# Layer 1 of a two-layer graph network: 64-row products in pairs, slice sums in four 64x64 quadrants, features moved to VectorE

## The chip, the cores and the metric

One NeuronCore of a Trainium2 chip runs the kernel. The metric is the device time in microseconds (us), median over the runs. The profile is of one execution, and its span runs from the first to the last instruction of that execution. Five engines matter: PE (TensorE), DVE (VectorE), ACT (ScalarE), POOL (GpSimd) and SP (SyncE, which only issues DMAs).

## The reference, cut to what matters

```python
# x (100000, 32), 25000 edges (src, dst), edge_weight, edge_attr_3
x = layernorm(x + L0(x, ...))            # scatter messages both ways, four tanh layers
x = layernorm(x + L1(x, edge_weight, edge_attr_3, edge_index))

def L1(features, abs_distances, rel_vec, edge_index, w1, b1, w2, b2):
    R = relu(abs_distances[:, None] @ w1 + b1) @ w2 + b2      # (E, 64) @ (64, 384): radial products
    Y = spherical_harmonics(rel_vec)
    Fj = features[src]                                        # 8 scalars and 8 vectors a row
    # for every block (i, j) and every k: sum over the 8 input channels v
    acc += NORM[i] * einsum('euv,ef,evi,ofi->euo', R[..., k], Y[lf], Fj[j], C)
    out = zeros.at[dst].add(msg)
```

## The kernel before, in words

The 25000 edges are padded to 196 tiles of 128 edges, one edge a partition. The stages before Layer 1 sort the edges, gather rows for Layer 0, walk the sorted tiles and run the four tanh layers. They end with x1, the input of Layer 1, stored to DRAM. After Layer 1 a last walk adds the first messages of each window of nodes, normalizes and stores.

Layer 1 takes the tiles in 28 groups (`NU`) of 7 (`U`). Each engine runs its own list in program order, and semaphores join the lists. For a group g:

- SP loads `arow` (each edge's weight, broadcast to 64 partitions), `load_weights`. ACT makes `ht` from it by one Relu, `hidden_3` (L738). A 65th row of `ht` is constantly 1.
- POOL gathers 7 times 128 rows of x1 by indirect DMA into `gat1`, `gather_3` (L566). It stands up to three groups ahead, as there are three buffers.
- ACT spreads the gathered rows into `feat5`, `fd` and `fk`, `features_3`. POOL makes three small products of `feat5` with the edge's direction, its own `features_3` (L577 to L579), and DVE reduces one and subtracts the others, `features_3` (L1389, L1390).
- PE makes the radial products: a tile is one product of `ht` (65 rows x 128 edges) with `rw` (65 x 384; row 65 is the bias), `radial` (L1018). Three PSUM banks take turns. ACT copies each to `rsb`, `radial_3`. There is one `rsb`, so the copies for group g+1 wait for DVE's products of group g.
- DVE multiplies `rsb` with `fd` and `fk`, `products_3` (L1397, and L1400 three times), into `prod`: 16 slices of 280 columns (7 tiles x 40).
- PE adds the 16 slices: 16 products of the 128x128 identity with a slice, accumulated in one bank of two, `sums` (L1025).
- ACT copies the sum out, `sums_3`. DVE builds the centred message and its payload, `message_3` (L1408 to L1420). PE multiplies it with the one-hot `oh1` that ACT makes (`away_from_3` L764, `hot_3` L769), `extras` (L1034). DVE adds the 7 results to `res`, `extras_3` (L1308).

The orders of the lists are: PE `radial(g+1)`, `sums(g)`, `extras(g-1)`; DVE `products_3(g)`, `features_3(g+1)`, `message_3(g-1)`, `extras_3(g-2)`; ACT `features_3(g+1)`, `radial_3(g+1)`, `away_from_3(g)`, `hidden_3(g+2)`, `hot_3(g)`, `sums_3(g)`.

An f32 product is one instruction in the program and two weight loads and two MATMUL records in the trace; a bf16 product is one of each.

## Time and profile before

| | |
|---|---|
| median of 3 runs | 1983.5 us (1983.34 to 1989.6) |
| the profiled execution, from first to last instruction | 1707.1 us |
| lies outside the profiled instructions (median less span) | 276.4 us |
| PE busy | 1315.9 us, 77% |
| DVE busy | 1193.5 us, 70% |
| POOL busy | 1068.9 us, 63% |
| ACT busy | 858.9 us, 50% |
| mean granted TensorE clock | 0.846 |

The profiled execution is known by its span alone. The rest of the measured time lies before the first and behind the last instruction, and a difference in the span is read as the same difference in the time. Busy shares are means over stages with different limits, so the rows below are taken by stretches. Layer 1 runs from about 1140 to 1560 us of the span. PE's clock has two levels, 2.4 GHz (1.00 in the rows) and 1.2 GHz (0.50), and a number between is a mean over a stretch.

### The profile page before, as it was taken

What the parts mean: (1) busy time and instruction counts of PE and PEld (TensorE: products, weight loads), DVE (VectorE), ACT (ScalarE), POOL (GpSimd) and SP (SyncE); (2) the same over time, 40 slices, a digit from 0 to 9 for tenths busy, and PEclk for the clock granted to TensorE, in tenths of its full rate; (3) what the DMA queues carried; (4) which work ended last, traced back from release to release, by engine and by line L of the source; (5) the groups of instructions that cost most, each with busy time, mean ns of one, the idle gap of its engine ahead of it and who ended that gap; (6) DMA issues with size and microseconds to landing.
All of it is one profiled execution on the core that took longest, in us unless ns stands there. A gap on an engine that the chain in (4) does not pass through costs nothing.

```text
span 1707.1 us, 25367 instructions
## 1 busy us (share of the span) xinstructions
PE 1315.9 (77%) x6200; PEld 957.6 (56%) x6200; DVE 1193.5 (70%) x3648; ACT 858.9 (50%) x2256; POOL 1068.9 (63%) x1168
## 2 busy tenths in 40 slices
PE   5699993686513777665778999958999999996673
PEld 1388881242212555554655666635777777775563
DVE  9699995677512443676667999964777777774776
ACT  0167770011101222666775777735666666664884
POOL 7777778777777777774111444448877887830444
PEclk8599996577555999888888999977999999997655
DMA  1000000123224988665555666531222222213785
GB/s 41 13 14 13 14 14 20 47 72 79 67 68 127 257 250 246 171 174 145 132 138 140 179 184 189 163 95 32 58 58 57 58 64 67 59 42 78 196 216 157
DMA packets 298498, 178.98 MB, mean 105 GB/s; under 512 B 28715, under 2 KB 290032, under 8 KB 298352
## 3 DMA queue, kind: packets, MB, share of 16 engines
q1 hardware_dynamic: 219712, 116.54, 26.0%
q0 software_dynamic: 29008, 36.18, 8.3%
q10 hardware_dynamic: 49632, 24.65, 5.0%
q8 instruction: 51, 0.84, 0.2%
q14 instruction: 95, 0.78, 0.2%
HBM read 111.18 MB, written 66.07 MB: 104 GB/s over the span
## 4 chain that ended last, share of the span: by engine, by line
PE 42%; POOL 28%; issue 16%; DVE 8%; DMA 2%; DVEq 2%; SPq 1%; ACT 1%; POOLq 0%; ACTq 0%
PE bank L1025 12%; POOL gat L511 12%; POOL lined L518 11%; PE bank L994 7%; PE bank L1018 7%; DVE res L1308 5%; PE bank L945 3%; POOL out L591 3%; PE bank L947 3%; PE bank L1034 3%; PE bank L1003 3%; PE bank L987 3%; DMA placed<-pay,pos_i 1%; DVEq L1308 1%; DVEq L1302 1%
## 5 line engine op out<-in xcount | busy, mean ns | idle before, releaser
L566 POOL DMA_INDIRECT gat<-x_d,src_i x196 | 253.2, 1292 | 59.0 <-issue 53.1
L511 POOL DMA_INDIRECT gat<-in_x,key_i x196 | 211.1, 1077 | 64.8 <-issue 62.4
L1308 DVE TENSOR_TENSOR res<-res,bank 128x128 f32 x588 | 168.4, 286 | 108.5 <-issue 24.4
L528 POOL DMA_INDIRECT placed<-pay,pos_i x196 | 191.9, 979 | 68.1 <-issue 65.6
L518 POOL DMA_INDIRECT lined<-in_x,other_i x196 | 195.8, 999 | 59.7 <-issue 59.7
L1025 PE MATMUL bank<-prod,ident 128*128 128x280 f32 x896 | 217.0, 400 | 0.0
L1025 PEld LDWEIGHTS bank<-prod,ident 128*128 128x128 f32 x896 | 171.0, 191 | 46.5 <-issue 0.6
L956 PE MATMUL bank<-woh,pw 128*128 128x128 f32 x784 | 135.4, 335 | 69.3 <-DVE woh L1287 33.4
L956 PEld LDWEIGHTS bank<-woh,pw 128*128 128x128 f32 x784 | 120.3, 238 | 85.5 <-DVE woh L1287 44.5
L56 ACT ACTIVATE xt<-bank 128x128 f32<-128x128 f32 x98 | 26.6, 271 | 269.6 <-PE bank L897 261.2
L1018 PE MATMUL bank<-rw,ht 65*128 65x384 f32 x392 | 141.3, 514 | 23.3 <-ACT ht L738 13.8
L553 POOL TENSOR_TENSOR hx<-hid,xin 128x512 f32<-128x512 f32 x49 | 62.0, 1264 | 136.2 <-ACT hid L724 136.2
L878 PE MATMUL bank<-tile_oh,sel 128*128 128x196 f32 x784 | 143.0, 337 | 3.1 <-ACT tile_oh L651 2.0
L878 PEld LDWEIGHTS bank<-tile_oh,sel 128*128 128x128 f32 x784 | 131.0, 193 | 17.3 <-issue 17.0
L1130 DVE SCALAR_TENSOR_TENSOR junk<-iota,w_f,bank 128x196 f32<-128x196 f32 x392 | 138.0, 408 | 0.9 <-PE bank L869 0.9
L994 PE MATMUL bank<-hid,wsl 128*128 128x512 f32 x294 | 134.9, 594 | 0.4 <-ACT hid L724 0.4
L56 ACT ACTIVATE rsb<-bank 128x384 f32<-128x384 f32 x196 | 95.5, 491 | 52.7 <-PE bank L1018 45.6
L1052 PE MATMUL bank<-pw,oh 128*128 128x128 f32 x392 | 89.6, 400 | 41.3 <-ACT oh L814 39.9
L689 ACT ACTIVATE woh<-iota,kr 128x128 f32<-128x128 f32 x294 | 93.8, 390 | 52.6 <-PE bank L956 26.0
L1018 PEld LDWEIGHTS bank<-rw,ht 65*128 65x128 f32 x392 | 75.8, 200 | 75.0 <-issue 17.9
L724 ACT ACTIVATE hid<-bank,bias 128x512 f32<-128x512 f32 x147 | 101.1, 688 | 31.2 <-PE bank L994 31.2
L1138 DVE TENSOR_TENSOR pay<-bank,wjs 128x512 f32<-128x512 f32 x49 | 33.8, 689 | 115.1 <-PE bank L902 115.0
(204 smaller groups left out, 2840.5 us busy)
## 6 DMA issues: line engine op xcount, KB each, us to landing
pw<-placed SPq DMA_DIRECT2D x588, 68.0 KB, 2.1
pw<-placed SPq DMA_DIRECT2D x98, 272.0 KB
xin<-in_x_t SPq DMA_DIRECT2D x53, 256.0 KB, 3.2
placed<-pay SPq DMA_DIRECT2D x49, 272.0 KB, 2.4
x_d<-res POOLq DMA_DIRECT2D x49, 256.0 KB, 3.8
placed<-pay SPq DMA_DIRECT2D x28, 448.0 KB, 3.2
out<-out ACTq DMA_DIRECT2D x49, 256.0 KB, 2.7
xin<-in_x_t ACTq DMA_DIRECT2D x45, 256.0 KB, 3.6
```

The costliest lines, as they stand in the source:

```text
L56: return act.activation(out, in_, ACT.Copy)
L511: pool.indirect_dma_start(gat[:, t, :], None, x, bass.IndirectOffsetOnAxis(ap=key_i[:, 0, t:t + 1], axis=0)).then_inc(s_gat, 16)
L518: pool.indirect_dma_start(lined[i % LINED][:, k, :], None, x, bass.IndirectOffsetOnAxis(ap=other_i[:, t:t + 1], axis=0)).then_inc(s_lined[ ...
L528: pool.indirect_dma_start(placed[1].rearrange("t p r -> (t p) r"), bass.IndirectOffsetOnAxis(ap=pos_i[:, 1, t:t + 1], axis=0), pay[i % 4][ ...
L566: pool.indirect_dma_start(gat1[g % 3][:, k, :], None, x1_d, bass.IndirectOffsetOnAxis(ap=src_i[:, t:t + 1], axis=0)).then_inc(c_gat[g % 3] ...
L878: ins = pe.matmul(psum[4 + 2 * v][:, 0:NT], sel[g % 2][:, k, v, :], tile_oh[g % 2][:, k, :], start=t == 0, stop=t == NT - 1)
L956: ins = pe.matmul(quarter(bank, k), pw[i % 6][:, k, 0:P], woh[i % 4][:, k, :], start=True, stop=True)
L994: pe.matmul(psum[BANK[n][h]][:, :], wsl[:, 2 + n, :], hid[n - 1][h][:, :], start=True, stop=True).then_inc(m_mm[n], 1)
L1018: pe.matmul(psum[n % 3][:, 0:RC], ht[g % 2][:, P * k:P * k + P], rw[:, :, :].rearrange("p a b -> p (a b)"), start=True, stop=True).then_in ...
L1025: ins = pe.matmul(psum[3 + g % 2][:, 0:40 * U].rearrange("p (t u) -> p t u", t=U), ident[:, :], prod[g % 2][:, :, v, :], start=v == 0, sto ...
L1130: dve.scalar_tensor_tensor(out=junk[n % 4][:, :], in0=iota[:, :], scalar=w_f[:, c, t:t + 1], in1=column(n), op0=ALU.is_equal, op1=ALU.mult ...
L1308: add.up(dve.tensor_tensor(into, into, quarter(bank + k // G, k % G), ALU.add))
```

## The change

The change touches Layer 1 and what feeds it.

- `arow`, `ht`, `rw` and the radial weights now stand on 128 partitions: even tiles of a group on partitions 0 to 63, odd ones on 64 to 127. `ht` is 128 x 512 instead of 64 x 896. The bias has no row of its own. It is split in three bf16 pieces, which lie on three rows of each half of `rb3`, and each tile gets one extra bf16 product of ones with `rb3` ahead of its f32 product. Four banks take turns.
- Each 128x128 identity product over a slice becomes two of the four 64x64 products: for a row half a and a column half b, the slice v + (a != b) goes to bank `SUMS[a]`, partitions of half b. What belongs to half a but landed on the other half is copied out by ACT (`crossed`) and brought back by two more 64x64 products, `cross`, which stand behind `extras(g-1)` on PE. Both banks belong to one group, so `sums(g)` waits for the copies of group g-1 rather than of g-2.
- POOL's three feature products move to DVE.
- DVE prepares `rb3` in the placement stage, where it already made `rw`. SP loads the weights of `rw` behind a wait for `s_rec`.

```diff
-            for g in range(NU + 1):
-                if g < NU:
-                    gather_3(g)
-                if g >= 1:
-                    features_3(g - 1)
+            for g in range(NU):
+                gather_3(g)
...
-                act.activation(ht[h][0:HID, :], arow[h][:, :], ACT.Relu, bias=rwc_sb[:, 1:2], scale=rwc_sb[:, 0:1]).then_inc(c_ht, 1)
+                act.activation(ht[h][:, :], arow[h][:, :], ACT.Relu, bias=rwc_sb[:, 1:2], scale=rwc_sb[:, 0:1]).then_inc(c_ht, 1)
...
             def sums_3(g):
                 act.wait_ge(c_sum, g + 1)
+                for a in range(2):
+                    ins = act_copy(act, crossed[HALVES[1 - a], :, :], summed(a, 1 - a))
+                ins.then_inc(c_cross, 1)
+                act.wait_ge(c_whole, g + 1)
                 wait(act, c_msg, g)
-                ps = psum[3 + g % 2][:, 0:40 * U].rearrange("p (t u) -> p t u", t=U)
-                act_copy(act, msg[:, :, 0:8], ps[:, :, 0:8])
-                act_copy(act, rest[:, :, :], ps[:, :, 8:40]).then_inc(c_scal, 1)
+                for a in range(2):
+                    act_copy(act, msg[HALVES[a], :, 0:8], summed(a, a)[:, :, 0:8])
+                    ins = act_copy(act, rest[HALVES[a], :, :], summed(a, a)[:, :, 8:40])
+                ins.then_inc(c_scal, 1)
...
             def radial(g):
                 pe.wait_ge(c_ht, g + 1)
-                for k in range(U):
-                    n = U * g + k
-                    wait(pe, c_rsb, n - 2)
-                    pe.matmul(psum[n % 3][:, 0:RC], ht[g % 2][:, P * k:P * k + P], rw[:, :, :].rearrange("p a b -> p (a b)"),
-                              start=True, stop=True).then_inc(c_r, 1)
+                for k in range(0, U, 2):
+                    pair = [(U * g + k + o, HID * o) for o in range(min(2, U - k))]
+                    for n, r in pair:
+                        wait(pe, c_rsb, n - 3)
+                        pe.matmul(psum[RADIAL[n % 4]][:, 0:RC], unit[r:r + HID, :], rb3[r:r + HID, :, :].rearrange("p a b -> p (a b)"),
+                                  start=True, stop=False)
+                    for n, r in pair:
+                        pe.matmul(psum[RADIAL[n % 4]][:, 0:RC], ht[g % 2][r:r + HID, P * (k // 2):P * (k // 2) + P],
+                                  rw[r:r + HID, :, :].rearrange("p a b -> p (a b)"), start=False, stop=True).then_inc(c_r, 1)
...
             def sums(g):
                 pe.wait_ge(c_prod, g + 1)
-                wait(pe, c_scal, g - 1)
-                for v in range(16):
-                    ins = pe.matmul(psum[3 + g % 2][:, 0:40 * U].rearrange("p (t u) -> p t u", t=U), ident[:, :], prod[g % 2][:, :, v, :],
-                                    start=v == 0, stop=v == 15)
+                wait(pe, c_scal, g)
+                for v in range(0, 16, 2):
+                    for b in range(2):
+                        for a in range(2):
+                            ins = pe.matmul(summed(a, b), ident[HALVES[a], HALVES[a]], prod[g % 2][HALVES[a], :, v + (a != b), :],
+                                            start=v == 0, stop=v == 14 and a != b)
                 ins.then_inc(c_sum, 1)
+            def cross(g):
+                pe.wait_ge(c_cross, g + 1)
+                for a in range(2):
+                    ins = pe.matmul(summed(a, a), ident[HALVES[1 - a], HALVES[1 - a]], crossed[HALVES[1 - a], :, :], start=False, stop=True)
+                ins.then_inc(c_whole, 1)
...
             def features_3(g):
                 h = g % 2
...
+                dve.wait_ge(c_feat, g + 1)
+                chain.up(dve.tensor_tensor(dprod[:, :, :, :], feat5[h][:, :, :, 0:3], along(0), ALU.mult))
+                chain.up(dve.tensor_tensor(kp[:, 0], feat5[h][:, :, :, 2:5], along(1), ALU.mult))
+                dve.tensor_tensor(kp[:, 1], feat5[h][:, :, :, 1:4], along(2), ALU.mult).then_inc(c_kp, 1)
+                done(chain)
+                dve.tensor_reduce(fd[h][:, :, 1, :], dprod[:, :, :, :], AX_X, ALU.add)
                 dve.wait_ge(c_kp, g + 1)
-                dve.tensor_reduce(fd[h][:, :, 1, :], dprod[:, :, :, :], AX_X, ALU.add)
```

PE's list before, from `radial(0)` on (`bank<-rw,ht` is a radial product, `bank<-prod,ident` a slice of the sums, `bank<-pay,oh` the extras):

```order
L1018 MATMUL bank<-rw,ht 128x384 x14
L1025 MATMUL bank<-prod,ident 128x280 x16
L1018 MATMUL bank<-rw,ht 128x384 x7
L1025 MATMUL bank<-prod,ident 128x280 x16
L1034 MATMUL bank<-pay,oh 128x128 x7
```

PE's list now, the whole of one later group (`bank<-rb,unit` is the bias, `bank<-crossed,ident` the halves brought back):

```order
L1032 MATMUL bank<-rb,unit 128x384 x2
L1035 MATMUL bank<-rw,ht 128x384 x2
L1032 MATMUL bank<-rb,unit 128x384 x2
L1035 MATMUL bank<-rw,ht 128x384 x2
L1032 MATMUL bank<-rb,unit 128x384 x2
L1035 MATMUL bank<-rw,ht 128x384 x2
L1032 MATMUL bank<-rb,unit 128x384
L1035 MATMUL bank<-rw,ht 128x384
L1044 MATMUL bank<-prod,ident 64x280 x32
L1059 MATMUL bank<-pay,oh 128x128 x7
L1051 MATMUL bank<-crossed,ident 64x280 x2
```

A group's 7 radial and 16 sum products became 14 and 32, and two products that wait for ACT stand at its end, ahead of the next group's radial products.

ACT's list now, from the one-hot of group g to the features of g+2 (before, the five rows from `crossed` to `rest` were the two copies `msg<-bank 128x7x8` and `rest<-bank 128x224`, and `ht` was 64x896):

```order
L778 ACTIVATE oh<-oh 128x896
L56 ACTIVATE crossed<-bank 64x280 x2
L56 ACTIVATE msg<-bank 64x7x8
L56 ACTIVATE rest<-bank 64x224
L56 ACTIVATE msg<-bank 64x7x8
L56 ACTIVATE rest<-bank 64x224
L56 ACTIVATE feat<-gat 128x56x3
L56 ACTIVATE feat<-gat 128x56x2
L56 ACTIVATE fd<-gat 128x7x8
L56 ACTIVATE fk<-gat 128x7x8 x3
L56 ACTIVATE rsb<-bank 128x384 x7
```

The wait for PE's `cross` lies between `crossed` and the first `msg`, and the features and the `rsb` copies of the next groups are queued behind it.

DVE's list now, between the products of two groups:

```order
L1462 TENSOR_TENSOR prod<-rsb,fk 128x112x8 x3
L1446 TENSOR_TENSOR dprod<-feat,rec 128x168
L1447 TENSOR_TENSOR kp<-feat,rec 128x168
L1448 TENSOR_TENSOR kp<-feat,rec 128x168
L1450 TENSOR_REDUCE fd<-dprod 128x7x8
L1452 TENSOR_TENSOR fk<-kp 128x7x8x3
L1470 TENSOR_TENSOR rq<-rest,rec 128x168
```

The three rows L1446 to L1448 are the ones that stood on POOL; before, L1389 (the reduction) followed `prod` directly.

## Rows read from the trace of the kernel before

**Rows 1.** Stretch: us, busy (count) of PE, PEld, DVE, ACT, POOL; PEclk, DMA, GB/s.

```profile
1200.00:1500.00 300.00, 300.00 (x1322) 226.69 (x1321) 220.69 (x399) 194.91 (x529) 237.82 (x221) 1.00 0.25 60
```

**Rows 2.** Chain that ended last, one group of Layer 1: start, us, what.

```profile
1269.88 7.55 PE bank L1025 x32
1277.42 1.56 PE bank L1034 x14
1278.98 4.52 PE bank L1018 x14
```

**Rows 3.** Waits, 1180 to 1540 us: total, times, longest.

```profile
ACT msg L56 <- PE bank L1025: 87.1, 27, 4.2
DVE fd L1389 <- POOL kp L579: 58.5, 26, 6.4
```

**Rows 4.** Timeline of DVE, one group: start, us, what.

```profile
1280.61 0.33 DVE L1389 TENSOR_REDUCE fd<-dprod 128x56 f32<-128x168 f32 x1 [1.93 <-POOL kp L579]
1280.85 0.43 DVE L1390 TENSOR_TENSOR fk<-kp 128x168 f32<-128x168 f32 x1
1281.13 0.31 DVE L1408 TENSOR_TENSOR rq<-rest,rec 128x168 f32<-128x168 f32 x1
...
1284.50 2.86 DVE L1308 TENSOR_TENSOR res<-res,bank 128x128 f32 x7 [0.70 <-issue]
1287.28 2.02 DVE L1397 TENSOR_TENSOR prod<-rsb,fd 128x1792 f32<-128x1792 f32 x1
1289.22 3.09 DVE L1400 TENSOR_TENSOR prod<-rsb,fk 128x896 f32<-128x896 f32 x3
1294.22 0.33 DVE L1389 TENSOR_REDUCE fd<-dprod 128x56 f32<-128x168 f32 x1 [1.91 <-POOL kp L579]
```

**Rows 5.** Timeline of PE at full clock in the sort, bf16 products.

```profile
183.26 0.33 PE L868 MATMUL bank<-oh,lower 128*128 128x392 bf16 x1
183.42 0.33 PE L869 MATMUL bank<-cum,pick 113*128 113x392 bf16 x1
```

**Rows 6.** Timeline of ACT, one group.

```profile
1277.46 0.22 ACT L56 ACTIVATE msg<-bank 128x56 f32<-128x56 f32 x1 [3.15 <-PE bank L1025]
1277.58 0.35 ACT L56 ACTIVATE rest<-bank 128x224 f32<-128x224 f32 x1
1277.81 0.57 ACT L56 ACTIVATE feat<-gat 128x168 f32<-128x168 f32 x2
...
1278.37 0.61 ACT L56 ACTIVATE fk<-gat 128x56 f32<-128x56 f32 x3
...
1282.25 0.49 ACT L56 ACTIVATE rsb<-bank 128x384 f32<-128x384 f32 x1 [0.15 <-PE bank L1018]
...
1283.93 2.14 ACT L764 ACTIVATE oh<-iota,kr 128x128 f32<-128x128 f32 x7
1285.97 1.12 ACT L738 ACTIVATE ht<-arow,rwc_sb 64x896 f32<-64x896 f32 x1
1287.00 0.94 ACT L769 ACTIVATE oh<-oh 128x896 f32<-128x896 f32 x1
```

**Rows 7.** Group of POOL's gathers, 1202 to 1529.3 us: busy, mean ns, idle before.

```profile
L566 POOL DMA_INDIRECT gat<-x_d,src_i x159 | 212.0, 1333 | 45.0 <-issue 42.7
```

**Rows 8.** Chain that ended last, start of Layer 1.

```profile
1163.60 2.02 DVE prod L1397
...
1174.69 8.61 PE bank L1025 x32
```

**Rows 9.** Chain that ended last, end of Layer 1.

```profile
1537.89 7.56 PE bank L1025 x32
...
1552.44 3.31 PE bank L1034 x14
```

**Rows 10.** Stretches in a walk of Layer 0 and in the placement, as in rows 1.

```profile
840.00:900.00 60.00, 42.16 (x234) 35.71 (x233) 41.05 (x147) 43.30 (x116) 9.79 (x56) 0.84 0.53 133
450.00:600.00 150.00, 64.72 (x295) 43.34 (x292) 45.15 (x154) 21.61 (x86) 113.90 (x118) 0.67 0.52 142
```

More of the change, by code:

```diff
@@ L147, in gnn_kernel @@
         bias = sb("bias", [P, 4])
-        rwc_sb = sb("rwc_sb", [HID, 2])
-        rw = sb("rw", [HID + 1, 16, 24])
+        rwc_sb = sb("rwc_sb", [P, 2])
+        rw = sb("rw", [P, 16, 24])
+        rb3 = sb("rb3", [P, 16, 24], BF16)
+        unit = sb("unit", [P, P], BF16)
         kr = sb("kr", [P, NT])
@@ L241, in gnn_kernel @@
         rest = sb3("rest", [P, U, D])
+        crossed = sb3("crossed", [P, U, 40])
         mean = sb3("mean", [P, U])
@@ L411, in gnn_kernel, with summed @@
         BACK = (5, 6, 7)
+        RADIAL = (0, 1, 2, 7)
+        SUMS = (3, 4)
+        HALVES = [slice(HID * a, HID * a + HID) for a in range(2)]
+        def summed(a, b):
+            return psum[SUMS[a]][HALVES[b], 0:40 * U].rearrange("p (t u) -> p t u", t=U)
         block = ctx.enter_context(nc.Block())
@@ L423, in _ @@
             sp.dma_start(bias[:, :], b0).then_inc(s_wld, 16)
-            sp.dma_start(rwc_sb[:, :], rwc).then_inc(s_wld, 16)
-            sp.dma_start(rw_raw[:, :], rwb).then_inc(s_wld, 16)
+            for h in range(2):
+                sp.dma_start(rwc_sb[HID * h:HID * h + HID, :], rwc).then_inc(s_wld, 16)
             sp.wait_ge(s_zero, 1)
@@ L432, in load_x @@
                 sp.dma_start(wins(xin[n % 4][:, :]), x_t[G * b:G * b + G].rearrange("w p q -> p w q")).then_inc(s_xin[n % 4], 16)
+            sp.wait_ge(s_rec, 1)
+            for h in range(2):
+                sp.dma_start(rw_raw[HID * h:HID * h + HID, :], rwb[0:HID, :]).then_inc(s_rwld, 16)
+                sp.dma_start(rb_raw[HID * h:HID * h + HID, :], rwb[HID:HID + 1, :].partition_broadcast(HID)).then_inc(s_rwld, 16)
             for q in range(NG):
@@ L479, in load_weights @@
                 wait(sp, c_ht, g - 1)
-                sp.dma_start(arow[h][:, :].rearrange("p (t q) -> p t q", t=U),
-                             ew_d[U * g:U * g + U, :].partition_broadcast(HID)).then_inc(c_arow[h], 16)
+                for o in range(2):
+                    n = (U + 1 - o) // 2
+                    sp.dma_start(arow[h][HID * o:HID * o + HID, 0:P * n].rearrange("p (t q) -> p t q", t=n),
+                                 ew_d[U * g + o:U * g + U:2, :].partition_broadcast(HID)).then_inc(c_arow[h], 16)
             def store_3(g):
@@ L1044, in _ @@
                     extras(g - 1)
+                if g < NU:
+                    cross(g)
             pe.wait_ge(c_scal, NU)
@@ new lines, in radial_weights @@
+            def radial_weights():
+                dve.wait_ge(s_rwld, 64)
+                dve.memset(unit[:, :], 1.0)
+                chain.up(combine(rw, rw_raw))
+                done(chain)
+                chain.up(combine(rb, rb_raw))
+                chain.up(dve.tensor_scalar(half[:, :], pcol[:, :], float(HID), -float(HID), ALU.is_ge, ALU.mult))
+                done(chain)
+                chain.up(dve.tensor_tensor(half[:, :], half[:, :], pcol[:, :], ALU.add))
+                done(chain)
+                for n in range(3):
+                    chain.up(dve.tensor_scalar(piece[:, n:n + 1], half[:, :], float(n), None, ALU.is_equal))
+                for n in range(3):
+                    chain.up(dve.tensor_copy(rb_h[:, :, :], rb[:, :, :]))
+                    done(chain)
+                    if n == 0:
+                        ins = dve.tensor_scalar(rb3[:, :, :], rb_h[:, :, :], piece[:, 0:1], None, ALU.mult)
+                    else:
+                        ins = dve.scalar_tensor_tensor(out=rb3[:, :, :], in0=rb_h[:, :, :], scalar=piece[:, n:n + 1], in1=rb3[:, :, :],
+                                                       op0=ALU.mult, op1=ALU.add)
+                    if n == 2:
+                        ins.then_inc(s_rw, 1)
+                    else:
+                        chain.up(ins)
+                        chain.up(dve.tensor_tensor(rb[:, :, :], rb[:, :, :], rb_h[:, :, :], ALU.subtract))
+                        done(chain)
```

73 lines of the change are left out of this document (36 added, 37 removed).

## The prediction, made before the result was known

> **What bounds the kernel now.** I read first the busy time by stretch. In Layer 1 PE is busy for all of 300 us at full clock, DVE for 220.7, ACT for 194.9, POOL for 237.8 [rows 1]. Since a busy PE can hide waits, I then took the chain that ended last: through all of Layer 1 it holds only PE's rows, 7.55 us of slice sums, 1.56 us of extras, 4.52 us of radial products, without a gap, 13.63 us a group [rows 2]. The waits say the same from the other side: ACT waits 87.1 us for the sums, DVE 58.5 us for POOL's feature products [rows 3]. Last, the timelines of the three others give what each needs of the 13.6 us once PE no longer sets them [rows 4, 6, 7]. Everything outside Layer 1 stays, so the question is the period of a group, times the 27 periods between the products of group 0 and of group 27.
>
> PE's prices are spacings, not the recorded durations: an f32 record of 280 columns takes 7.55 / 32 = 0.236 us, one of 384 takes 4.52 / 14 = 0.323 us [rows 2], a bf16 record of 392 takes 0.165 us although it is shown with 0.33 [rows 5].
>
> **PE, part by part.** Two 64-row products stand on different rows of the array, four 64x64 products on different quarters. No row of this kernel shows two products at once in parts of the array, so the price of a part has two ends: a share of a full record (0.236 / 4 = 0.059 us for a quarter's record, 0.323 / 2 for a half's), or the full record.
> - Sums: 32 products, 64 records. At 0.059 that is 3.8 us (saves 3.8), at 0.236 it is 15.1 us (costs 7.6).
> - Radial: 7 f32 products, now 4 turns instead of 7. A turn is 0.165 for the bias and 2 x 0.323, so 0.81, four are 3.2 us (saves 1.3); with no overlap 7 x 0.81 = 5.7 us (costs 1.2).
> - Cross: 2 products, 2 x 0.236 = 0.47 us if they overlap, 0.94 if not.
> - Changes of the array's division, four a group: between nothing and the 0.165 us by which a record outlasts its spacing [rows 5], so 0 to 0.7 us; I take 0.5.
>
> With full overlap PE works 3.2 + 3.8 + 1.56 + 0.47 + 0.5 = 9.5 us a group, and is no longer the bound. I take full overlap, since each of the four products in a turn has its own rows or columns, its own bank or its own half of one, and 64 columns of weights in place of 128.
>
> **DVE.** From the reduction at 1280.61 to the last of the prod rows at 1289.22 + 3.09 = 1292.31 there is no wait but 0.70 us of issue: 11.70 us. Then it waits 1.91 us for POOL, and the period is 13.61 us [rows 4]. The wait goes; three products of 168 columns come. The nearest rows are 0.31 and 0.43 us long for 168 columns, and follow each other by 0.24 and 0.28 us [rows 4]. Three take between 0.72 and 1.3 us. I take 0.9. DVE needs 11.7 + 0.9 = **12.6 us** a group. This is late next.
>
> **ACT and the loop through PE.** A group's `rsb` copies start at a moment X, when DVE's products end. PE has four banks full, and needs copies 0 and 1 (0.49 us each [rows 6]) for its next pair: that ends at X + 1.0 + 0.8, the last single at X + 2.6, the sums at X + 6.5, extras at X + 8.0. ACT meanwhile: 7 copies to 3.6, one-hot 2.14 to 5.7, `ht` with 512 columns instead of 896, about 0.7, to 6.4, the Relu 0.94 to 7.4 [rows 6]. `crossed` is two copies of 280 columns, between the 0.35 of 224 and the 0.49 of 384, less overlap, 0.7: X + 8.1. PE's cross and its result 0.6: 8.7. The halved `msg` and `rest` take twice the 0.35 us of today, since a copy's columns and not its partitions count: 9.4. Features 1.17 us (1277.81 to 1278.98 [rows 6]): 10.6, with the 0.5 us of changes about **11.1 us**. Only then may the next `rsb` copies start. That is 1.5 us under DVE's 12.6, so the added wait is hidden as long as the sums take no more than 3.8 + 1.5 = 5.3 us; from 6.3 us on the period is longer than today's.
>
> **POOL.** 7 gathers of 1.333 us and 0.30 of issue are 11.4 us [rows 7]; the three feature products leave. The gathers are stretched beside DVE's products; were all of DVE's new 0.9 us added to them, 12.3, still under 12.6. SP's two loads in place of one are issued in time it idles.
>
> **The clock.** PE waits about 3 us a group now. In a walk where PE is busy 42.2 of 60 us, its mean clock is 0.84, so a third of the stretch ran at 1.2 GHz [rows 10]. PE would be busy 9.5 / 12.6 = 75% here. A third of a period at half clock adds up to 2.1 us to PE's part of the loop, 11.1 to 13.2, and nothing if it falls where PE is ahead. I take 0.3 us on the period: **12.9 us** (ends 12.6 and 13.5).
>
> **Ends of the stage, and the rest.** The first products stand behind POOL's features, which stand behind the gathers of group 1; they start at 1163.60 [rows 8]. DVE alone can start when the `rsb` copies are in, some 3 us earlier (0 to 3.5). At the end 7.56 us of sums start 1 us after the products [rows 9]; now 3.8, then extras, cross and copies: 2 us less (0 to 3). DVE's preparation of `rb3` is about 25 small instructions, at most 12 us, in a stretch of 150 us in which DVE works 45 and POOL 114 [rows 10]: POOL's DMAs hide it; zero. Uncovered it would cost those 12 us.
>
> **Sum.** (13.63 - 12.9) x 27 = 19.7, plus 3, plus 2 = 24.7 us. The span goes from 1707.1 to 1682.4. The median stands 276.4 us above the span, and nothing there changes, so 1983.5 - 24.7 = **1959 us**. This case's own range: at 12.6, 27.8 + 6.5 = 34 less, 1949; at 13.4, with 3 of gain at the ends, 1974.
>
> **Rivals.**
> 1. *Only neighbours overlap* (slower). An f32 product is two records on the same part of the array. If PE starts its records strictly in program order, the second record of a product waits for its first, and the next product's first starts beside it: one f32 product per 0.236 us, whatever the number of parts. 32 products take 7.55 us, the same as today, and the loop is X + 2.9 for radial (a pair is 0.165 + 3 x 0.323), 10.4 for the sums, 11.2 `crossed`, 12.0 extras, 12.9 cross (3 x 0.236 and the result), 13.6 the copies, 14.8 the features, 15.2 with changes. (15.2 - 13.63) x 27 = 42 us, less 2 at the ends: **2024 us**. For it: the doubled records [rows 2] are back to back and every product here has two; against it: nothing shows yet that a record on another part must wait. It decides from sums of 6.3 us on. The Trainium skill, "TensorE: Matmul & The Clock Gate", Part 3, says that MATMULs start and end in program order, and only weight loads are pulled ahead; by that rule, applied to two-record products, this rival would hold. The same section gives 4 tiles about 3 times the throughput, for products that are not doubled. No run here shows either yet.
> 2. *No overlap at all* (slower): radial tail 3.3, sums 15.1, then cross, copies and features as above, 23 us a group: 9.4 x 27 = 253, **2235 us**. For it: every record of today's trace on one engine is a full turn; against it: the parts share neither rows, columns nor bank.
> 3. *The clock eats it* (no change). PE's waits bring it to half clock just where the sums start; the loop becomes 13.5 to 14 us. At 13.8: 4.6 more, 5 less at the ends, **1983 us**. For it: rows 10. Against: a slow PE waits less, and today's Layer 1 came back to full clock after the 8.61 us sums of its start [rows 8] and stayed there [rows 1].
> 4. *Partial overlap*: sums of 6.5 to 7 us by weight loads that don't hide (64 loads now for 32). Loop near 14.2: 15 us more, less 5: **1994 us**.
>
> **Chances.** Forecast 0.48, rival 1 0.27, rival 2 0.06, rival 3 0.10, rival 4 0.09. A difference of under 0.3%, 6 us, can't be told from none. Faster by more: the forecast and a share of rival 3, 0.51. Within 0.3%: 0.07. Slower: 0.42. The range reaches from the forecast's lower end, 1949, to rival 1 with half a period's 0.3 us on top, 2032; it leaves out rival 2 and little else.
>
> **What would show it.** PE's records of a sum phase: 64 within 3.8 us (forecast) or 7.5 (rival 1) or 15. A DVE without waits between its groups and a period of 12.6 to 12.9, against ACT's `rsb` copies waiting no longer for DVE but following its features directly, with DVE waiting for `rsb` (rivals 1 to 4). PEclk under 0.9 in Layer 1 for rival 3. First products near 1160. If DVE's three products take over 1.3 us or the gathers over 1.8 us each, the forecast fails without PE.

## The result, and what it depends on

| | before | changed | ratio, 95% interval |
|---|---|---|---|
| the comparison that scores the prediction | 1986.55 us | 2062.62 us | 1.0392 (1.0376 to 1.0408) |
| the same two kernels on another chip | 1704.38 us | 1659.53 us | 0.9732 (0.9715 to 0.9748) |

The change was forecast at 1959 us and came out at 2062.62 us: slower by 3.9%. (One of the four runs of the kernel before, of 2395.32 us, was slow and does not count in the ratio.) On another chip the change is faster by 2.7%. The experiments met five chips, and they fall into two kinds. On three of them (here **kind A**) the kernel before takes 1986 to 1993 us, on the other two (**kind B**) 1704 to 1707 us. Each chip was met in one session only, so whether a kind belongs to the chip or to a condition that it was in is not shown. The times of the first comparison agree with kind A. The profile of before, with its span of 1707.1 us, agrees with kind B, and all rows ahead of the prediction are from it. The "276.4 us outside the span" were never outside it: in the other profiles the time is 1.8 to 2.8 us above its span. They are stages ahead of Layer 1 that are longer on kind A. Between the two profiles of before, one of each kind, the sort adds 170 us (POOL's next gathers start at 447.8 instead of 277.5 us), and the gathering and placing behind it add 102 more (the last row is placed at 1063.7 instead of 791.7 us).

Here are 150 us of the sort, in the kernel before on kind B and then on kind A (columns as in [rows 1]).

```profile
100.00:250.00 150.00, 147.34 (x838) 125.37 (x837) 150.00 (x759) 106.73 (x296) 112.88 (x113) 1.00 0.09 14
```

```profile
100.00:250.00 150.00, 28.50 (x80) 17.86 (x80) 21.77 (x91) 10.30 (x32) 111.77 (x116) 0.53 0.09 13
```

POOL is issuing its indirect gathers at the same pace (113 and 116 instructions), but PE, DVE and ACT get through a tenth to an eighth of their instructions beside them. On kind A they catch up after POOL has finished, at 261.7 us: from 350 to 450 us PE does 539 instructions.

### The profile page after: what moved, and what is told of

It reads as the page before. It is cut to its first block, busy times and chain, and to the rows that moved or that the text cites. A ratio compares the mean times of both kernels' runs of the same rounds, so it can differ in the third digit from the quotient of the medians.

```text
span 2057.6 us, 27913 instructions
## 1 busy us (share of the span) xinstructions
PE 1342.4 (65%) x7404; PEld 890.1 (43%) x7404; DVE 1227.8 (60%) x3753; ACT 872.7 (42%) x2368; POOL 987.5 (48%) x1084
## 4 chain that ended last, share of the span: by engine, by line
PE 33%; DVE 24%; issue 22%; another core or an unknown queue 9%; POOL 3%; ACT 3%; DVEq 2%; SPq 2%; DMA 1%; POOLq 0%; ACTq 0%
PE bank L1044 8%; PE bank L1008 6%; DVE res L1361 5%; DVE junk L1157 5%; DVE oh L1127 4%; DVE sel L1229 4%; PE bank L1059 3%; PE bank L959 3%; PE bank L1001 2%; PE bank L961 2%; POOL out L600 2%; PE bank L1017 2%; PE bank L1035 2%; SPq L390 1%
## 5 line engine op out<-in xcount | busy, mean ns | idle before, releaser
L590 POOL DMA_INDIRECT gat<-x_d,src_i x196 | 227.5, 1161 | 200.3 <-ACT fk L56 144.3
L535 POOL DMA_INDIRECT gat<-in_x,key_i x196 | 196.4, 1002 | 64.9 <-issue 62.5
L1044 PE MATMUL bank<-prod,ident 64*64 64x280 f32 x1792 | 177.5, 438 | 60.2 <-issue 56.9
L882 PE MATMUL bank<-oh,lower 128*128 128x392 bf16 x196 | 78.5, 401 | 173.9 <-DVE junk L1157 80.8
L892 PE MATMUL bank<-tile_oh,sel 128*128 128x196 f32 x784 | 153.5, 350 | 26.6 <-issue 24.7
L56 ACT ACTIVATE pos_i<-pos_f 128x4 int32<-128x4 f32 x98 | 20.1, 205 | 336.4 <-DVE junk L1157 259.4
L1044 PEld LDWEIGHTS bank<-prod,ident 64*64 64x64 f32 x1792 | 81.8, 140 | 149.7 <-issue 121.9
L1165 DVE TENSOR_TENSOR pay<-bank,wj 128x512 f32<-128x512 f32 x49 | 33.8, 690 | 155.7 <-remote 69.2
L1229 DVE TENSOR_SCALAR sel<-iota,rt_f,val 128x128 f32<-128x128 f32 x196 | 66.8, 341 | 99.6 <-remote 73.7
L882 PEld LDWEIGHTS bank<-oh,lower 128*128 128x128 bf16 x196 | 20.9, 106 | 218.3 <-issue 164.5
```

The source lines that it names most:

```text
L535: pool.indirect_dma_start(gat[:, t, :], None, x, bass.IndirectOffsetOnAxis(ap=key_i[:, 0, t:t + 1], axis=0)).then_inc(s_gat, 16)
L590: pool.indirect_dma_start(gat1[g % 3][:, k, :], None, x1_d, bass.IndirectOffsetOnAxis(ap=src_i[:, t:t + 1], axis=0)).then_inc(c_gat[g % 3] ...
L882: pe.matmul(pair_of(n), lower[:, :], oh[:, t:t + 2, :].rearrange("p t w -> p (t w)"), start=True, stop=False)
L892: ins = pe.matmul(psum[4 + 2 * v][:, 0:NT], sel[g % 2][:, k, v, :], tile_oh[g % 2][:, k, :], start=t == 0, stop=t == NT - 1)
L1044: ins = pe.matmul(summed(a, b), ident[HALVES[a], HALVES[a]], prod[g % 2][HALVES[a], :, v + (a != b), :], start=v == 0, stop=v == 14 and a ...
L1229: ins = dve.tensor_scalar(sel[g % 2][:, k, v, :], iota[:, 0:P], rt_f[g % 3][:, 0, k:k + 1], values[:, t:t + 1], ALU.is_equal, ALU.mult)
```

## The profile after

Layer 1 in the changed kernel on kind A, then the kernel before on kind A, then the changed kernel on kind B. They answer to [rows 1].

```profile
1500.00:1800.00 300.00, 237.78 (x1861) 131.08 (x1859) 194.59 (x382) 169.53 (x507) 148.24 (x127) 0.91 0.21 49
```

```profile
1500.00:1800.00 300.00, 300.00 (x1323) 226.62 (x1322) 220.54 (x397) 194.81 (x529) 236.38 (x219) 1.00 0.25 60
```

```profile
1200.00:1450.00 250.00, 208.01 (x2099) 121.29 (x2091) 217.81 (x427) 190.20 (x568) 183.79 (x153) 0.99 0.30 68
```

Before, kind A costs Layer 1 nothing: the row is that of [rows 1], and the steady period is 13.6 us on both kinds. Changed, PE is idle for a fifth of the time on kind A, and nobody else is the bound: DVE works 194.6 of 300 us, POOL 148.2.

PE's timeline of one group, changed kernel, kind A (start, us, line, operation, [idle before <- what ended it]):

```profile
1551.87 3.05 PE L1044 MATMUL bank<-prod,ident 64*64 64x280 f32 x46
1555.32 0.43 PE L1044 MATMUL bank<-prod,ident 64*64 64x280 f32 x1 [0.39 <-issue]
1556.74 0.42 PE L1044 MATMUL bank<-prod,ident 64*64 64x280 f32 x1 [0.99 <-issue]
1558.14 2.70 PE L1044 MATMUL bank<-prod,ident 64*64 64x280 f32 x16 [0.98 <-issue]
1560.77 2.74 PE L1059 MATMUL bank<-pay,oh 128*128 128x128 f32 x14
1563.44 0.69 PE L1051 MATMUL bank<-crossed,ident 64*64 64x280 f32 x4
...
1568.88 1.41 PE L1044 MATMUL bank<-prod,ident 64*64 64x280 f32 x20
```

The same on kind B:

```profile
1258.53 4.00 PE L1044 MATMUL bank<-prod,ident 64*64 64x280 f32 x64
1263.54 1.80 PE L1059 MATMUL bank<-pay,oh 128*128 128x128 f32 x14 [1.01 <-DVE res L1361]
1265.27 0.69 PE L1051 MATMUL bank<-crossed,ident 64*64 64x280 f32 x4
...
1270.95 4.00 PE L1044 MATMUL bank<-prod,ident 64*64 64x280 f32 x64
```

The four quarters do overlap, on both kinds: 46 records in 3.05 us here, 64 in 4.00 us there (3.85 us from the first start to the last, plus one spacing). In the raw records four starts stand about 7 ns apart, every 0.236 us, which is the spacing of one full record in [rows 2]. But on kind A PE stops 2.66 us after the sums began, at record 45 to 48 of 64, and starts the next ones 1.4 us apart, with nothing in the profile that it waits for ("issue"). The clock falls behind the stop and not ahead of it, as the stretches before, in and after it show (columns as in [rows 1]):

```profile
1551.87:1554.50 2.63, 2.63 (x44) 1.72 (x46) 2.19 (x5) 2.63 (x10) 1.90 (x2) 1.00 0.16 41
1554.50:1558.10 3.60, 1.28 (x8) 0.30 (x3) 3.03 (x6) 1.55 (x3) 2.94 (x3) 1.00 0.76 184
1558.10:1563.40 5.30, 5.22 (x30) 3.29 (x29) 3.10 (x4) 0.80 (x2) 0.91 (x1) 0.68 0.04 6
```

POOL's timeline of the same stretch:

```profile
1549.54 0.95 POOL L590 DMA_INDIRECT gat<-x_d,src_i  x1 [6.91 <-ACT fk L56]
1550.79 0.95 POOL L590 DMA_INDIRECT gat<-x_d,src_i  x1 [0.30 <-issue]
...
1555.81 0.95 POOL L590 DMA_INDIRECT gat<-x_d,src_i  x1 [0.30 <-issue]
1557.06 1.95 POOL L590 DMA_INDIRECT gat<-x_d,src_i  x1 [0.30 <-issue]
1566.55 0.95 POOL L590 DMA_INDIRECT gat<-x_d,src_i  x1 [7.54 <-ACT fk L56]
```

Seven gathers run from 2.3 us before the sums to 7.1 us into them, and PE runs freely again when they are over. The sums took 7.9 to 8.9 us in 20 of the 28 groups. In groups 24 to 26, when no gather is left, they took 3.85 us. (Group 27 took 5.5, on both kinds: its clock was 0.50 meanwhile, a cause of its own.) The waits of 1490 to 1850 us on kind A (total, times, longest) show what follows from it:

```profile
POOL gat L590 <- ACT fk L56: 136.2, 21, 7.7
...
ACT crossed L56 <- PE bank L1044: 98.3, 21, 5.2
DVE dprod L1446 <- ACT fk L56: 93.9, 21, 5.3
...
PE bank L1044 <- issue: 49.8, 80, 1.2
```

ACT waits for PE, DVE and POOL for ACT. POOL's wait (before, nearly all of its idle time was its own issue, [rows 7]) starts its seven gathers anew in each period just ahead of the sums, where they do most harm.

## The experiments

All times are medians; "sums of a group" is what most of the steady groups take, and "sums 0 to 27" the time from the first record of the first sum phase to the first record of the last one. A ratio stands where the kernel before ran several times beside it.

| kernel | chip | sums of a group | sums 0 to 27 | time | ratio to before there |
|---|---|---|---|---|---|
| before | A | 7.55 | 364.3 | 1992.5 (one run) | 1 |
| changed | A | 7.9 to 8.9 | 442.3 | 2062.6 | 1.0392 |
| e1 no gathers from group 3 on | A | 3.85 | 331.9 | 1950.7 (one run) | |
| e2 no SP traffic from group 2 on | A | 7.6 to 8.8 | 442.6 | 2059.6 (one run) | |
| e3 features on DVE | A | 7.55 | 374.7 | 1998.7 | 1.0057 (1.0040 to 1.0075) |
| e5 paired radial, features on DVE | A | 7.65 | 365.2 | 1980.8 | 0.9967 (0.9950 to 0.9984) |
| e8c four then three | A | 3.85 to 6.1 | 352.8 | 1970.2 (one run) | |
| e8d the same | A | 4.4 to 6.2 | 353.6 | 1982.8 | 0.9949 (0.9932 to 0.9966) |
| e7c gathers after the sums | A | 5.5 to 6.9 | 353.2 | 1984.5 | 0.9966 (0.9939 to 0.9992) |
| e10 one group later | A | 5.5 to 6.4 | 345.6 | 1978.2 | 0.9912 (0.9881 to 0.9943) |
| e9b plain DMAs | A | 3.85 | 329.9 | 1945.7 (one run) | |
| before | B | 7.55 | 363.3 | 1704.4 and 1707.1 | 1 |
| changed | B | 3.85 | 326.7 | 1659.5 | 0.9732 (0.9715 to 0.9748) |
| e4 paired radial | B | 7.65 | 349.6 | 1692.6 | 0.9911 (0.9879 to 0.9944) |
| e5b paired radial, features on DVE | B | 7.65 | 346.8 | 1679.6 | 0.9860 (0.9840 to 0.9880) |
| e7 gathers after the sums | B | 3.85 | 326.8 | 1667.6 | 0.9771 (0.9739 to 0.9804) |
| e8 four then three | B | 3.85 | 326.6 | 1665.4 | 0.9760 (0.9727 to 0.9794) |
| e8b the same | B | 3.85 | 329.7 | 1659.7 | 0.9727 (0.9706 to 0.9749) |
| e9 plain DMAs | B | 3.85 | 326.7 | 1658.2 (one run) | |

### What holds PE back: e1 and e2

e1 leaves out the gathers of groups 3 to 27 (the messages of those groups are computed from old rows):

```diff
-            for g in range(NU):
+            for g in range(3):
                 gather_3(g)
...
-                act.wait_ge(c_gat[g % 3], 16 * U * (g // 3 + 1))
+                act.wait_ge(c_gat[g % 3], 16 * U)
```

> The changed kernel with POOL's gathers of groups 3 to 27 left out (their rows are those of groups 0 to 2 again). Theory G, POOL's gathers hold back PE's record stream: the sums take 3.85 us in every group from 3 on and the period is 12.5 to 12.8 us, as in the three last groups of the changed kernel, where the gathers were over. Theory S, SP's store and loads do it: nothing changes, sums of 8.5 us and periods of 17 us. Theory B, a stretch of 46 products at full rate uses up a supply that refills slowly: nothing changes either.

e2 leaves out SP's stores of the payload and its loads of the weights from group 2 on (the output lacks them):

```diff
-                if g + 1 < NU:
+                if g + 1 < 2:
...
-                if g >= 2:
-                    store_3(g - 2)
```

> The changed kernel with SP's stores of the payload and its loads of the edge weights left out from group 2 on (448 and 224 KB a group less). Theory S: sums of 3.85 us and a period near 12.6 us. Theories G and B: the stall after 2.66 us of sums stays, sums of 8 to 8.7 us, period 16.5 to 17 us; under G it may shorten by what the gathers land sooner.

Without gathers the sums take 3.85 us in 24 of 28 groups, and sums 0 to 27 take 110 us less. Without SP's traffic, on the same chip, nothing changes, down to the stop after 2.66 us. So POOL's gathers hold PE back, and neither SP's transfers nor the length of the burst alone does.

### The parts of the change without the quarters: e3, e5, e4, e5b

e3 is the kernel before with POOL's three feature products on DVE, e5 adds the paired radial products, e4 is the pairing alone. In all, the sums are the 16 full products:

```diff
-                    for b in range(2):
-                        for a in range(2):
-                            ins = pe.matmul(summed(a, b), ident[HALVES[a], HALVES[a]], prod[g % 2][HALVES[a], :, v + (a != b), :],
-                                            start=v == 0, stop=v == 14 and a != b)
+                    ins = pe.matmul(psum[3 + g % 2][:, 0:40 * U].rearrange("p (t u) -> p t u", t=U), ident[:, :], prod[g % 2][:, :, v, :],
+                                    start=v == 0, stop=v == 15)
```

> The kernel before with POOL's three feature products moved to DVE and nothing else. PE is still needed for 13.63 us a group and DVE for 12.6, so the move alone is worth nothing but the 0 to 3 us of an earlier start: within 6 us of before. If DVE's three products cost more than the 1 us worked out (rival), the period goes above 13.7 us.

> The change without its quadrants: paired radial products and DVE's features stay, the slices are summed by 16 full-width identity products again. PE needs 3.2 + 7.55 + 1.56 us, so 12.4 to 12.9 us a group with changes of division, DVE 12.6 by the rows of before. If the stalls inside the sums are what cost the change its time (theory), nothing of them is left here, since no four products run at once: period 12.6 to 12.9 us against 13.63, and 20 to 32 us less than the kernel before. If the paired radial products or the three products on DVE are to blame (rival), the period stays above 13.6 us and the time is that of before or more.

> The paired radial products alone: features on POOL as before, sums with the full 128x128 identity. If four turns of a pair take 3.2 us instead of 4.5, PE needs 7.55 + 1.56 + 3.2 = 12.3 us a group and is no longer the bound alone; POOL with its 11.4 us of gathers and its three feature products (DVE waited 1.9 us a group for them) is then the next. Theory (POOL's products are the next bound): period 13.3 to 13.7, time within 6 us of before, 1978 to 1990. Rival (PE alone was the bound): period 12.6 to 12.9, 1957 to 1966.

> The same kernel as e5_paired_radial_dve_features (paired radial products, features on DVE, full 128x128 sums). On a quick chip its period stays at about 12.95 us but its start is not stretched: (13.63 - 12.95) x 27 = 18 us, and 0 to 3 at the start, so 1684 to 1690 us, ratio 0.987 to 0.99, and the changed kernel is about 18 us quicker than it. On a slow chip 1980 as before.

Full sums never stalled on either kind. Their stream is half as dense: 32 records in 7.55 us against 64 in 3.85. With the pairing the period is 12.96 us on both kinds, and e4 has it in most groups with POOL's features still in place (seven have 13.1 to 13.9), so PE was the bound, and the theory for e4 that POOL's products come next was wrong. e5 and e3 miss their forecasts on kind A: e5 gains 6 us instead of 20 to 32, and e3 loses 12 where it was to stay within 6. e5b gains 25 us on kind B, where 14 to 20 were forecast.

The start of the stage is what differs. e3 keeps the period of 13.6 us, as it must, and is slower on kind A by 0.6%: its first three sum phases start at 1441.9, 1464.5 and 1480.4 us, 38.5 us for two groups against 28.2 in the kernel before there (1458.7 to 1486.9). In e5 it is 44.8 us. The timelines of POOL show a difference: the kernel before interrupts its gathers for its three feature products after the first 14 and after each 7 more, while e5 issues 35 in an unbroken row. With the products off POOL nothing separates the gathers any more, and on kind A the start of the stage lies beside them. In e5 ACT is held up there. PE and then ACT:

```profile
1446.41 9.26 PE L1037 MATMUL bank<-prod,ident 128*128 128x280 f32 x32
1470.93 0.22 ACT L56 ACTIVATE msg<-bank 128x56 f32<-128x56 f32 x1 [15.07 <-remote]
```

The sums that ACT copies here ended at 1455.67 us, and ACT stood idle until 1470.93, with nothing of this core named that it waited for. The row of 35 gathers ended at 1468.49. On kind B (e5b) the same copy starts as soon as the sums end. That this costs e3 and e5 their time is an inference: no run separates the gathers again, and the profiled run of e3 is the fastest of its eight. On kind B, e5b starts its sums at 1155.6, 1169.0 and 1182.0 us: 26.4 us.

### Does the order matter: e7, e8 and the two kernels again

e7 adds one wait to the changed kernel, e8 puts the wait between the fourth and the fifth gather:

```diff
             def gather_3(g):
                 wait(pool, c_feat, g - 2)
+                wait(pool, c_sum, g - 3)
                 for k in range(U):
```

```diff
                 for k in range(U):
+                    if k == 4:
+                        wait(pool, c_sum, g - 3)
                     t = U * g + k
```

> The kernel before, unchanged, for a profile of the same kind as those of the other runs. The profile shown of before has a span 276 us under its median, that of the changed kernel one that is only 5 us under its median. If what lies outside the span is small for every run (theory: the profiled execution of before had a quicker sort stage), this span is near 1980 us, the first radial product of Layer 1 starts near 1419 us instead of 1144 us, and the period of a group is 13.6 us as before. The rival, that 276 us lie outside the span of this kernel, gives a span near 1707 us. It also gives the start of Layer 1 in a run with the slow sort stage: if the 17 us that the two runs with the features on DVE spent more in the first two groups come from that, here too sums 0 to sums 2 take 38 to 45 us rather than 27.

> The changed kernel with one more wait: POOL issues the seven gathers for group n+4 only when the sums of group n are done, so that a burst of gathers starts behind a sum phase and is over, or nearly, by the next one (7 x 1.33 us = 9.3 of about 12.7 us). Theory G (the gathers issued during the sums hold PE back, from the fifth one after a pause on): sums 3.85 us in nearly all groups, period 12.6 to 13.2, 1940 to 1965 us. Rival (the hold-up is tied to how many gathers are issued in a period, wherever they stand): sums stay near 8 us, or the radial products take the stall instead, period 16 to 17, near 2060.

> The changed kernel, but POOL issues only the first four gathers of a group where it does now (they start 2.3 us ahead of the sums) and the other three only when the running sums are done. Theory G5 (PE is held up only once the fifth gather after a pause starts, at 2.7 us of the sums): sums 3.85 us in nearly all groups, period 12.6 to 13.2, 1940 to 1965 us, like the run with all seven behind the sums. Rival G1 (any gather beside the sums holds them back, after 2.7 us of a dense stream): sums still near 7 to 8 us, period 16 to 17, near 2060, while the run with all seven behind the sums is quick.

These four runs fell on a chip of kind B: the kernel before took 1707.1 us there, with the first radial products where the profile ahead of the prediction has them. Both kernels had sums of 3.85 us, which looked like a success of the theory and was none, because gathers still stood beside the sums in all but the last groups (in most at -2.5, -1.2, 0.0, 1.3, 2.5 and 3.8 us of them). So the changed kernel itself had to be run on that kind.

> The changed kernel, unchanged. The last four runs fell on a chip (or a condition of it) in which the kernel before takes 1707 us at the median, as in the profile shown of before; the first ones on one in which it takes 1986, with a sort stage 275 us longer while POOL gathers. Theory C (the hold-up of PE beside POOL's gathers belongs to that slow condition, not to the kernel): where the kernel before takes 1707 here, the changed kernel has sums of 3.85 us, a period near 12.4 and takes 1662 to 1672 us, ratio 0.975 to 0.98; where it takes 1986, 2060 as before. Rival K (the order of gathers and sums in the kernel makes the stall on any chip, and the pacing of the last two runs took it away): on the quick chip too sums near 8 us, period 17 and 1775 to 1790 us, ratio about 1.04.

> The same kernel as e8_four_then_three (the last three gathers of a group wait for the running sums), beside the changed kernel on one chip. On a quick chip theory C expects it within 0.3% of the changed kernel, rival K about 110 us quicker. On a slow chip (before at 1986) theory G5 expects sums of 3.85 us and 1940 to 1965 us; if any gather beside the sums holds PE back there, sums stay near 8 us and it takes about 2060.

The changed kernel has sums of 3.85 us there too, and pacing is worth nothing (1659.5 and 1659.7 us). Theory C holds, rival K falls: the hold-up goes with the kind, and not with the kernel alone.

### The gathers' making or their traffic, on kind A: e9 and e9b

```diff
-                    pool.indirect_dma_start(gat1[g % 3][:, k, :], None, x1_d,
-                                            bass.IndirectOffsetOnAxis(ap=src_i[:, t:t + 1], axis=0)).then_inc(c_gat[g % 3], 16)
+                    pool.dma_start(gat1[g % 3][:, k, :], x1_d[P * t:P * t + P, :]).then_inc(c_gat[g % 3], 16)
```

(from group 3 on; the rows are those of the tile in order and not the indexed ones, so the messages are others.)

> The changed kernel with the gathers of groups 3 to 27 replaced by plain DMAs of the same size from POOL (7 a group, 128 rows of 128 bytes each, in order instead of by index, so the messages are other ones). It tells on a slow chip whether POOL's making of the indirect DMAs or their traffic holds PE back: with theory D (the making of them) sums 3.85 us and 1945 to 1955 us as without gathers, with theory Q (the traffic of small rows) sums near 8 us and about 2060. On a quick chip both expect what the changed kernel takes, less up to 8 us.

> The kernel of e9_plain_dma once more (the gathers of groups 3 to 27 replaced by plain DMAs of the same size from POOL, so the messages are other ones), for the slow condition: theory D (POOL's making of the indirect DMAs holds PE back) gives sums of 3.85 us and 1945 to 1955 us, theory Q (the traffic of small rows does) sums near 8 us and about 2060. In the quick condition 1658 as before.

> The kernel of e8_four_then_three once more, for the slow condition (the kernel before at 1986 us): theory G5, in which PE is held up only once the fifth gather after a pause starts, gives sums of 3.85 us in nearly all groups and 1940 to 1965 us; if any gather beside the sums holds PE back, sums stay near 8 us and it takes about 2060. In the quick condition (before at 1705) it repeats 1660 to 1666.

> The kernel before, unchanged, for a profile in the slow condition: the span is then near its time, 1983, the sort stage 275 us longer than in the profile shown, Layer 1's period 13.63 us. Its sums of 7.55 us should show no stall (theory: only a dense stream of records is held up, and theirs is half as dense), and its first two groups take 38 to 45 us if the stretched start of the two runs with the features on DVE comes from the condition. In the quick condition it repeats 1707.

e9 told nothing, as it fell on kind B. The last three ran on kind A. The same number of transfers of the same size, issued plainly, leaves the sums alone (3.85 us in 24 of 28 groups, the others at a fallen clock). PE and then POOL in e9b:

```profile
1552.93 4.00 PE L1047 MATMUL bank<-prod,ident 64*64 64x280 f32 x64
```

```profile
1550.39 3.71 POOL L594 DMA_DIRECT2D gat<-x_d  x7 [8.70 <-ACT fk L56]
```

Theory D fits: POOL's making of the indirect DMAs holds PE back, and transfers of that number and size do not. One rival is left. The plain DMAs read their rows in order, and a packet of that queue takes 45 ns at the mean instead of 79 ns with the gathers, so reads in the order of an index were taken away too. Against it stands that the gathers' packets take 78 ns on kind B as well, where nothing stops. No run makes plain DMAs of scattered rows. The changed kernel itself was not run on this chip, but e8c was, and it has stops. Before_b shows 7.55 us sums without a stop beside the same gathers.

Theory G5 fell. e8c took 1970 us and not 2062, but stops remained in most groups, some with no gather starting between 1.4 us into the sums and their end (groups 8, 12 and 13: last gather started at 1.3 to 1.4 us, stop at 2.66). It is not the fifth gather.

### Pacing on kind A: e7c, e8d, e10

e10 is e7 with `g - 2` in place of `g - 3`.

> The changed kernel in which POOL issues the gathers for group n+3 only when the sums of group n are done (one group later than in e7), so that those of group 3 no longer run beside the first sums. In the slow condition the supply theory (POOL's making of an indirect DMA slows what reaches PE; 45 to 50 records of a dense stream are there in advance, the rest is late as long as gathers go on) gives: first sums 6 to 8 us instead of 24.7, later ones 3.85 to 5.5, period 12.4 to 13.0, 1945 to 1962 us. If seven gathers (9.3 to 11 us and their landing) don't fit between the end of one group's sums and the features behind the next one's, the period is 13.5 and more and the time above 1975. In the quick condition 1658 to 1665, and above 1690 if they don't fit.

> The kernel of e7_gathers_after_sums once more. In the slow condition the supply theory expects sums of 3.85 to 5.5 us, as with four then three, and fewer gathers past 2.7 us of the sums, so 1955 to 1970 us; the first sums are still stretched to 14 us or more by the gathers of group 3. In the quick condition 1660 to 1668 as before.

> The kernel of e8_four_then_three with rounds, for an interval against the kernel before. In the slow condition 1970 as in the one run there, ratio 0.99 to 0.995; in the quick condition 1660 to 1666, ratio 0.973 to 0.976.

PE in one group of e10:

```profile
1536.53 3.51 PE L1045 MATMUL bank<-prod,ident 64*64 64x280 f32 x51
1540.27 0.39 PE L1045 MATMUL bank<-prod,ident 64*64 64x280 f32 x1 [0.23 <-issue]
1541.02 1.18 PE L1045 MATMUL bank<-prod,ident 64*64 64x280 f32 x12 [0.36 <-issue]
```

A wait of one line takes the loss in the steady groups from 4.7 to about 1.7 us (the stops alone, at a clock of 1.00), and the period from 17.0 to 12.8 us. The changed kernel was not run on this chip either: its 17.0 us and 2062.6 us come from other chips of the kind, and the difference of some 80 us is far above what separates those (6 us for the kernel before). All three now beat the kernel before on kind A, but by under 1%, e10 by 0.9%. The rest stays because seven gathers take 9.3 us and more, and a period of 12.4 us leaves 8.5 between two sum phases. The first two groups, 43.1 us long in the changed kernel and 49.7 in e2, take 26.2 in e10 (23.0 on kind B); in e7c and e8d they still take 33.5 and 38.8. The times are all above their forecasts (1945 to 1962 for e10, 1955 to 1970 for e7c, 1970 for e8d): the steady sums take 5.5 us and more where 3.85 was hoped for, and the stages ahead of Layer 1 ended some 10 us later in these runs than in the first ones (first gather of Layer 1 at 1432.6 us against 1417.8), which the kernels compared there share. e7 and e8 are ahead of the kernel before on both kinds (e8 0.973 to 0.976 on kind B, where it is level with the changed kernel, and 0.995 on kind A). e10 has the lowest time on kind A, 1978.2 against 1982.8 for e8d with intervals that overlap, and was not run on kind B.

## Why the prediction was wrong, and what in it was right

**The step that failed** is the one that let the gathers run beside the sums at no cost: in the part on POOL they were weighed only as load on POOL (11.4 us, "still under 12.6"), and in the part on PE "full overlap" made a stream twice as dense as any f32 stream of [rows 2], priced by PE's array alone. What brings the records to PE was taken to be free. On kind A PE's records come late beside indirect gathers: the sums took 8.55 us instead of 3.85, and 3.85 again without gathers (e1) or with plain DMAs in their place (e9b). The profile ahead of the prediction could not show that, since it is of kind B, but one number could have warned: 276 us between the span and the median of the runs. I explained them away as lying outside the profiled instructions. A gap of 14% asks whether profile and times are of the same condition.

**The loop worked out for PE and ACT** holds. It gave 11.1 us with sums of 3.8 us. On kind A the sums take 4.7 us more (some 3.6 of stops, the rest at half clock), and the extras behind them, still at half clock, 1.1 more (from 1560.77 to 1563.44, 2.67 us instead of 1.56). That makes 16.9 us; measured 17.0. The decision point, put at sums of 5.3 us, lies at about 5.1: in e8c and e10 sums of 4.4 us leave the period at 12.4 to 12.5, sums of 5.5 make it 12.8 and sums of 6.1 make it 13.4, a microsecond for a microsecond. Above it ACT waits for PE, and DVE for ACT.

**The account of kind A.** Against before_b: to the first gather of Layer 1 10.3 us less (a mark that lies anywhere from 1413 to 1433 us in the eleven profiles of that kind), from there to the first sums 4.6 less, sums 0 to 27 78.0 more, the rest 3.8 more: 66.9 us of span, and 76 us of the medians. Of the 78.0, 17.5 are between sums 0 and sums 1 (32.0 us against 14.5), the rest in the periods of 17 us.

**The account of kind B**, on which the working was based. The forecast was 24.7 us less; it is 44.9 less by the medians and 47.6 by the spans of before_again and after_again: 7.6 ahead of Layer 1 (a mark that differs by 15 us among runs there, nothing that the change touches can be named), 5.2 at the start (forecast 3), 36.7 in the periods (forecast 19.7), and 2.0 more at the end (forecast 2 less; the last sums ran at a clock of 0.50, which cost 1.7 us).

- *Full overlap*: right. The Trainium skill, "TensorE: Matmul & The Clock Gate", Part 3, has MATMULs start and end in program order. Here four starts stand within about 20 ns, and then a spacing later the next four. The records name neither their product nor their quarter, so whether they keep the program's order can't be read from them. What fails is rival 1's cap of one product a turn: 32 products would have taken 7.5 us, and took 3.85. Rivals 2 and 4 have no run for them either.
- *Radial*, *crossed*, *cross*, *halved msg and rest*: as forecast or close to it. A pair's turn takes 0.82 us (forecast 0.81), the two `crossed` copies 0.81 (0.7), PE's cross and its result 0.74 (0.6), and `msg` and `rest` with half the partitions 0.21 and 0.34, as long as before with all of them. The changes of the array's division, priced at 0.5 us a group, cost little: the first spacing behind one is 0.34 instead of 0.236 us ahead of full sums (e5) and 0.29 ahead of quarters (after_again). PE's timeline:

```profile
1265.89 0.34 PE L1032 MATMUL bank<-rb,unit 64*128 64x384 bf16 x2
1266.07 0.81 PE L1035 MATMUL bank<-rw,ht 64*128 64x384 f32 x4
1266.71 0.33 PE L1032 MATMUL bank<-rb,unit 64*128 64x384 bf16 x2
```

- *DVE*: three products follow each other by 0.25 us, 0.74 in place of 0.9. The period in which DVE sets the end is 12.37 us in three groups of four and 11.8 in the fourth, 12.2 at the mean, instead of 12.6. The timeline of DVE on kind B, which answers to [rows 4]:

```profile
1268.25 0.33 DVE L1446 TENSOR_TENSOR dprod<-feat,rec 128x168 f32<-128x168 f32 x1
1268.50 0.33 DVE L1447 TENSOR_TENSOR kp<-feat,rec 128x168 f32<-128x168 f32 x1
1268.75 0.32 DVE L1448 TENSOR_TENSOR kp<-feat,rec 128x168 f32<-128x168 f32 x1
...
1272.89 2.87 DVE L1361 TENSOR_TENSOR res<-res,bank 128x128 f32 x7 [0.70 <-issue]
...
1277.62 3.09 DVE L1462 TENSOR_TENSOR prod<-rsb,fk 128x896 f32<-128x896 f32 x3
1280.62 0.33 DVE L1446 TENSOR_TENSOR dprod<-feat,rec 128x168 f32<-128x168 f32 x1
```

- *The clock*: no cost on kind B, 0.99 in the window above, although PE waits 17% of it. The 0.3 us were wrong there, and rival 3 with them. On kind A it is 0.91: it falls behind each stop and costs about 1.1 us in the sums and 1.1 in the extras of a group, as much as the 2.1 us that the part on the clock gave as the most, but behind the stops, which no rival had.
- *The chances*: slower had 0.42, but for reasons none of which came true. No rival named the supply of a dense stream.

## What to carry to other kernels

A denser PE stream can be held up where a sparser one was not; look for what else runs in those microseconds, indirect gathers first, even if they load no shared engine. Where the profile's span and the median of the runs differ by more than the 1.8 to 2.8 us seen here, find the stage that differs before working anything out from the profile. And an experiment that shows a cure must have the sick kernel beside it on the same chip: e7 and e8 looked like one where nothing was ill, and e7c, e8d and e10 stand beside the kernel before alone.

## What the runs showed of the hardware

- Four f32 products of 64 rows by 64 columns on the four quarters of the array run together: 64 records in 3.85 us, where 32 full ones take 7.55.
- The five chips seen fall into two kinds (or conditions). On one, the other engines get through few instructions while POOL makes indirect DMAs: in the sort PE did 80 records in 150 us instead of 838. That the gathers are the reason there too is not shown, as no run of the sort leaves them out. The longer stages cost the kernel before 284 us ahead of Layer 1 (first gather there at 1428.1 instead of 1144.1 us).
- On that kind a dense PE stream mostly goes on for 45 to 52 records and then gets single ones 0.7 or 1.4 us apart; a stream of one f32 record in 0.236 us never stopped. ACT was held up too, for 15 us beside an unbroken row of gathers (e5). Plain DMAs from POOL, as many and as large, do no harm.
- Open: by what way POOL's work reaches the other engines (8 of the 20 groups with these stops have no transfer of the instruction queues beside their sums), whether the order of the gathered rows plays a part, why the kinds differ, and why a few groups beside gathers were free (group 12 of the changed kernel, 3.85 us; groups 9, 20 and 22 of e10). In those one gather, started about 0.5 us into the sums, took 2.0 us instead of 1.25, so fewer were made; that was seen and not tried.
